# Start-up of a two-layer kernel: loads on two queues sorted by first use, the first tile's steps written ahead of the loops, weight pieces four tiles later, two accumulations of a pair tile in flight

## The reference

```python
x = x + attn(layernorm(x))     # delta-rule linear attention, 4 heads, key 128, value 64
x = x + ffn(layernorm(x))      # mixture of 8 experts, 2 chosen per token, hidden 1024
# attn: q, k = x@Wq, x@Wk; v, g = x@Wv, x@Wg; beta = sigmoid(x@Wb); k = k/|k|; q = q*128**-0.5
#   per token t: S = S + k_t (beta_t (v_t - k_t^T S))^T ; o_t = q_t^T S
#   o = rmsnorm(o) * norm_w * silu(g);  result o @ Wo
# ffn: probs = softmax(x @ router^T), top 2; sum over both of prob * gelu(x @ w1[e]^T) @ w2[e]^T
```

## Time and profile before

| | |
|---|---|
| median of three executions | 976.61 us (975.64 to 978.22) |
| profiled execution | 973.25 us, span 971.4 us |
| PE busy | 855.0 us (88%) |
| DVE busy | 628.9 us (65%) |
| ACT busy | 601.8 us (62%) |
| POOL busy | 425.5 us (44%) |
| mean granted TensorE clock | 0.962 of 2.4 GHz |

### The profile page before, as it was taken

The page is one execution under the profiler, slowest core; times in us unless marked ns, Lnnn a source line. Parts: engine busy times, 40 slices in busy tenths (PEclk is TensorE's granted clock), DMA queues, the critical chain, the costliest instruction groups (busy, mean ns, idle before and its releaser), DMA issues. The chain is left out here.

```text
span 971.4 us, 29866 instructions
## 1 busy us (share of the span) xinstructions
PE 855.0 (88%) x9998; PEld 671.8 (69%) x9999; DVE 628.9 (65%) x1822; ACT 601.8 (62%) x1636; POOL 425.5 (44%) x426
## 2 busy tenths in 40 slices
PE   0589999999999999999971699999999999998983
PEld 0368887788878877788751577777777777766762
DVE  3468888898989989898846354555555554534341
ACT  4578888898888888877642454455445544534430
POOL 3445555667767766754536023232323232222122
PEclk9999999999999999999965699999999999999997
DMA  5212222233233323211106123233232323222212
GB/s 196 66 50 87 64 73 89 79 100 100 84 96 99 106 82 92 88 46 46 46 34 220 56 39 48 47 53 51 44 49 44 59 44 50 45 46 41 39 18 28
DMA packets 49736, 66.58 MB, mean 69 GB/s; under 512 B 6416, under 2 KB 34192, under 8 KB 49616
## 3 DMA queue, kind: packets, MB, share of 16 engines
q1 hardware_dynamic: 35616, 46.33, 16.3%
q0 software_dynamic: 13424, 18.10, 10.7%
q10 hardware_dynamic: 576, 0.53, 0.2%
HBM read 41.46 MB, written 23.48 MB: 67 GB/s over the span
## 5 line engine op out<-in xcount | busy, mean ns | idle before, releaser
L646 POOL DMA_INDIRECT out<-wvg_s,yidx x71 | 113.7, 1601 | 317.7 <-DVE wvg_s L1911 169.0
L934 PE MATMUL ps<-w_s,wqk 128*128 128x128 f16 (+1 forms) x1336 | 240.0, 288 | 11.7 <-ACT wqk L663 9.0
L934 PE MATMUL ps<-x_s,w_hi 128*128 128x256 f16 (+1 forms) x1376 | 201.2, 256 | 0.1
L934 PE MATMUL ps<-x_s,w_lo 128*128 128x256 f16 (+1 forms) x688 | 170.2, 255 | 0.0
L1884 DVE SCALAR_TENSOR_TENSOR KpAT<-KQ,wqk 128x512 f16<-128x512 f32 (+1 forms) x144 | 98.7, 686 | 100.5 <-ACT wqk L663 100.4
L663 ACT ACTIVATE w_s<-ps 128x512 f16<-128x512 f32 (+2 forms) x288 | 147.8, 532 | 25.6 <-PE ps L934 10.4
L934 PE MATMUL ps<-w_s,KpAT 128*128 x568 | 155.7, 274 | 0.0
L934 PEld LDWEIGHTS ps<-w_s,wqk 128*128 128x128 f16 x1336 | 101.7, 98 | 77.9 <-issue 14.7
L934 PEld LDWEIGHTS ps<-x_s,w_hi 128*128 x1376 | 120.4, 98 | 18.4 <-issue 0.8
L663 ACT ACTIVATE x_s<-ps 128x512 f16<-128x512 f32 x36 | 21.5, 596 | 163.6 <-PE ps L1310 163.6
L910 ACT ACTIVATE KQ<-ps 128x512 f32<-128x512 f32 (+1 forms) x144 | 85.1, 591 | 48.1 <-PE ps L934 42.3
(11 more groups left out here) (185 smaller groups left out, 1792.0 us busy)
## 6 DMA issues: line engine op xcount, KB each, us to landing
wst<-w SPq DMA_DIRECT2D x56, 256.0 KB, 2.8
w_s<-eye SPq DMA_DIRECT2D x32, 256.0 KB, 2.7
rowA<-routed_rows SPq DMA_DIRECT2D x28, 260.0 KB, 2.7
x_s<-x SPq DMA_DIRECT2D x32, 128.0 KB, 2.6
out<-x_s SPq DMA_DIRECT2D x32, 128.0 KB, 1.7
rowA<-routed_rows SPq DMA_DIRECT2D x15, 130.0 KB, 2.1
KQ<-w SPq DMA_DIRECT2D x6, 256.0 KB
out<-wvg_s,yidx POOLq DMA_INDIRECT x71, 3.9
```

Source lines behind the costliest of these rows:

```text
L646: pool.indirect_dma_start(out=out, out_offset=bass.IndirectOffsetOnAxis(ap=yidx[:, q, a:a + 1], axis=0), in_=yrow[:, q % 2, a, :], in_offs ...
L934: return pe.matmul(dst, lhsT, rhs, start=start, stop=stop, **kw)
```

## The change

- Loads go out on two queues. ACT issues `wk` and `wvg` before anything else. SP issues x tile 0, `fc`, `wb`, `wq`, x tile 1, `norm_w` (once, repeated on the host), `wo`, the masks (int8 on the host, straight into place), identity block 0, x tile 2, `router`, three identity loads that fill `Y`, identity block 1, x tile 3, identity block 2.
- Each constant has a semaphore of its own, and each wait stands where it is first needed.
- The first tile's layer norm, its evacuation and the layer norm of tile 1 stand in the preludes, ahead of or between the weight parts. The spare rows are written in POOL's loop step 4.
- The weight order is wk, wq, wvg, wo. All piece steps are four loop steps later.
- The casts and scaled constants of DVE come after the low parts of wk and wq.
- In phase B, the first expert tile's `up` is cut in two around the second tile's transposes, and the second half of a pair tile no longer waits for its first half's accumulation.

```diff
@@ SP
             load_x(0)
-            for dst, src in early + late_consts:
-                sp.dma_start(dst, src).then_inc(s_const, 16)
-            for n, (dst, src) in enumerate(weights):
-                sp.dma_start(dst, src.rearrange("(k p) n -> p k n", p=P)).then_inc(s_wload[n], 16)
+            sp.dma_start(fc[:, 0:FCONST], fconst).then_inc(s_fc, 16)
+            sp.dma_start(wb_in[:, :, :], wb.rearrange("(k p) n -> p k n", p=P)).then_inc(s_wb, 16)
+            sp.dma_start(wq_in, wq.rearrange("(k p) n -> p k n", p=P)).then_inc(s_wload[1], 16)
             load_x(1)
+            sp.dma_start(normw_s[:, :], norm_w).then_inc(s_normw_in, 16)
+            sp.dma_start(wo_in, wo.rearrange("(k p) n -> p k n", p=P)).then_inc(s_wload[3], 16)
+            sp.dma_start(mask_s[:, :, :], iconst).then_inc(s_mask, 16)
+            init_inverse(0)
             load_x(2)
+            sp.dma_start(router_s[:, :, :], router.rearrange("(k p) n -> p k n", p=P)).then_inc(s_router, 16)
+            for n in range(RING):
+                sp.dma_start(Y[:, 2 * n:2 * n + 2, :, :].rearrange("p l h n -> p (l h n)"), eye).then_inc(s_Yi, 16)
+            init_inverse(1)
             load_x(3)
-            for n in range(RING):
-                init_inverse(n)
+            init_inverse(2)
...
-                piece(2 * (i - 2) + 1)
-                piece(2 * (i - 1) + 0)
+                piece(2 * (i - 6) + 1)
+                piece(2 * (i - 5) + 0)
@@ POOL
-            pool.memset(S[:, :, :, :], 0.0).then_inc(s_init, 1)
-            pool.wait_ge(s_const, 16 * CONST_LOADS)
+            pool.wait_ge(s_fc, 16)
...
+            ln1_scale(0)
+            ln1_scale(1)
             for i in range(T + POOL_SKEW):
+                if i == 4:
+                    spare_rows()
                 ln2_scale(i - 5)
-                split_lo(2 * (i) + 0)
+                split_lo(2 * (i - 4) + 0)
                 scatter(i - 12, 1)
-                ln1_scale(i)
+                next_scale(i)
...
-                    value = i * 128 + (32 * q + 16 * a)
+                    value = i * 128 + (32 * q + (16 * a if split(i, q) else 0))
@@ ACT
-            act.wait_ge(s_const, 16 * CONST_LOADS)
+            act.dma_start(wk_in, wk.rearrange("(k p) n -> p k n", p=P)).then_inc(s_wload[0], 16)
+            act.dma_start(wvg_in, wvg.rearrange("(k p) n -> p k n", p=P)).then_inc(s_wload[2], 16)
+            ln1(0)
+            act.wait_ge(s_wb, 16)
             evac(wb_s[:, 0, :, :], wb_in[:, :, :], A_SCALE)
-            evac(Y[:, :, :, :].rearrange("p v h n -> p (v h) n"),
-                 ident.unsqueeze(1).broadcast_to([P, (LEVELS - 1) * H, P])).then_inc(s_Yi, 1)
+            xnT_evac(0)
             weight_hi(0, wk_s[:, 0, :, :], wk_in)
-            weight_hi(1, wvg_s[:, 0, :, :], wvg_in)
-            weight_hi(2, wq_s[:, 0, :, :], wq_in)
+            weight_hi(1, wq_s[:, 0, :, :], wq_in)
+            ln1(1)
+            weight_hi(2, wvg_s[:, 0, :, :], wvg_in)
...
-                scale_piece(2 * (i - 1) + 0)
+                scale_piece(2 * (i - 5) + 0)
...
@@ PE
-            pe.wait_ge(s_const, 16 * CONST_LOADS)
-            pe.wait_ge(s_init, 2)
-            pe.wait_ge(s_Yi, 1)
-            pe.wait_ge(s_wsh, 1)
-            pe.wait_ge(s_wsl, 1)
+            pe.wait_ge(s_fc, 16)
...
             xT_make(0, 0)
+            up(0, 0, range(0, 4))
             xT_make(0, 1)
-            up(0, 0)
+            up(0, 0, range(4, KH))
@@ DVE
-            dve.wait_ge(s_const, 16 * CONST_LOADS)
-            dve.wait_ge(s_init, 1)
+            dve.wait_ge(s_fc, 16)
+            ln1_stats(0)
+            xnT_low(0)
+            weight_lo(0, wb_s, wb_in[:, :, :])
+            weight_lo(0, wk_s, wk_in).then_inc(s_wsl, 1)
+            ln1_stats(1)
+            dve.wait_ge(s_normw_in, 16)
+            dve.tensor_scalar(normw_s[:, :], normw_s[:, :], A_SCALE, None, ALU.mult).then_inc(s_normw, 1)
+            weight_lo(1, wq_s, wq_in).then_inc(s_wsl, 1)
+            step(dve.tensor_copy(posI[:, :], ident))
+            step(dve.tensor_scalar(negI[:, :], ident, -1.0, None, ALU.mult))
             step(dve.tensor_copy(before16[:, :], before_neg))
             step(dve.tensor_copy(ones16[:, :], ones))
-            step(dve.tensor_copy(posI[:, :], ident))
-            step(dve.tensor_scalar(negI[:, :], ident, -1.0, None, ALU.mult))
+            step(dve.tensor_copy(run[:, :], region))
             settled()
             step(dve.tensor_scalar(before_neg, before_neg, -K_SCALE ** -2, None, ALU.mult))
             step(dve.tensor_scalar(causal, causal, 1.0 / K_SCALE, None, ALU.mult))
-            dve.tensor_scalar(normw_s[:, :], normw_s[:, :], A_SCALE, None, ALU.mult).then_inc(s_normw, 1)
-            step(dve.tensor_copy(mask_s[:, :, :].rearrange("p a b -> p (a b)"), mask_in))
-            link(dve.tensor_copy(run[:, :], region))
+            settled()
             dve.sem_inc(s_init, 1)
-            ln1_stats(0)
-            dve.wait_ge(s_Yi, 1)
-            weight_lo(0, wb_s, wb_in[:, :, :])
-            weight_lo(0, wk_s, wk_in).then_inc(s_wsl, 1)
-            weight_lo(1, wvg_s, wvg_in).then_inc(s_wsl, 1)
-            weight_lo(2, wq_s, wq_in).then_inc(s_wsl, 1)
+            weight_lo(2, wvg_s, wvg_in).then_inc(s_wsl, 1)
             dve.wait_ge(s_normw, 1)
             weight_lo(3, wo_s, wo_in, normw_s[:, 0:1]).then_inc(s_wsl, 1)
```

More of the change, by code:

```diff
@@ L246, in build @@
         p_yo = [PS[5 + a][:, :].rearrange("p (v n) -> p v n", v=2) for a in range(2)]
-        s_const = sem("const_loaded")
-        s_wload = [sem(f"{n}_loaded") for n in ("wk", "wvg", "wq", "wo")]
+        s_fc = sem("constants_loaded")
+        s_wb = sem("wb_loaded")
+        s_mask = sem("level_masks_loaded")
+        s_router = sem("router_loaded")
+        s_normw_in = sem("norm_weight_loaded")
+        s_wload = [sem(f"{n}_loaded") for n in ("wk", "wq", "wvg", "wo")]
         s_wsh = sem("attention_weight_hi")
@@ L416, in _ @@
         def _(sp):
[L417 to L421, removed]
             def load_x(n):
@@ L613, in scatter, with spare_rows, next_scale @@
                     in_=rowA[:, g % RG * C + c, :], in_offset=None).then_inc(s_scat[g % RG][c], 16)
[L615 to L621, removed]
+            def spare_rows():
+                pool.memset(rowA[:, C:2 * C, :], 0.0).then_inc(s_spare, 1)
+                pool.wait_ge(s_spare, 1)
+                pool.tensor_scalar(rowA[:, C:2 * C, D + 3], rowA[:, C:2 * C, D + 3], lane, float(B * N), ALU.add, ALU.add).then_inc(s_spare, 1)
+                pool.wait_ge(s_spare, 2)
+                for c in range(C):
+                    part = c % 2 * 64
+                    pool.dma_start(routed[SPARE + 64 * c:SPARE + 64 * (c + 1), :], rowA[part:part + 64, C + c, :]).then_inc(s_spared, 16)
+            def next_scale(n):
+                if n > 1:
+                    ln1_scale(n)
+            ln1_scale(0)
+            ln1_scale(1)
             for i in range(T + POOL_SKEW):
+                if i == 4:
+                    spare_rows()
                 ln2_scale(i - 5)
-                split_lo(2 * (i) + 0)
+                split_lo(2 * (i - 4) + 0)
                 scatter(i - 12, 1)
-                ln1_scale(i)
+                next_scale(i)
                 o_rsqrt(i - 4)
-                split_lo(2 * (i) + 1)
+                split_lo(2 * (i - 4) + 1)
                 kscale_(i - 1)
@@ L898, in xT_hi, with hidden @@
                 evac(xTh[:, q % 2, :, :], p_gT).then_inc(s_gTh, 1)
-            def hidden(i, q):
-                for m in range(4):
+            def hidden(i, q, ms=range(4)):
+                for m in ms:
                     act.wait_ge(s_hps, i * 16 + (4 * q + m + 1))
@@ L914, in _ @@
             xT_hi(0, 0)
+            hidden(0, 0, range(0, 2))
             xT_hi(0, 1)
-            hidden(0, 0)
+            hidden(0, 0, range(2, 4))
             def expert_body(i):
@@ L1323, in parts_of, with up @@
                 return [(expert_of(i, q), slice(0, PE_TOK))]
-            def up(i, q):
+            def up(i, q, ms=range(KH)):
                 owners = parts_of(i, q)
@@ L1329, in up @@
                 hi, lo = xTh[:, q % 2, :, :], xTl[:, q % 2, :, :]
-                for m in range(KH):
+                for m in ms:
                     if m % 2 == 0 and not (isinstance(i, int) and i * 4 + q < 1):
@@ L1507, in y_masked @@
                 done(dve, s_yps[q], n // 2, 7, lev + 1)
+                if n == 0 and lev == 1:
+                    dve.wait_ge(s_Yi, 16 * RING)
                 hold(dve)
@@ L1813, in _ @@
                 expert_masks(i - 8)
-                xnT_low(i - 2)
+                next_xnT_low(i - 2)
                 v_gate(i - 3)
@@ L1878, in xT_lo, with hidden_lo @@
                 dve.tensor_tensor(xTl[:, q % 2, :, :], p_gT, xTh[:, q % 2, :, :], ALU.subtract).then_inc(s_gTl, 1)
-            def hidden_lo(i, q):
-                for m in range(4):
+            def hidden_lo(i, q, ms=range(4)):
+                for m in ms:
```

(5 more changed lines are left out.)

47 lines of the change are left out of this document (31 added, 16 removed).

## The result

The changed kernel took 963.22 us (961.45 to 965.0, four runs), the kernel before 977.34 us in the same comparison: 14.1 us less, ratio 0.9853 [0.9832, 0.9874]. The forecast was 960.9. In two later comparisons, on other chips, the changed kernel took 968.56 us against 980.80 and 969.36 against 979.73, ratios 0.9876 [0.9861, 0.9891] and 0.9898 [0.9881, 0.9916]. So 10 to 14 us is the gain, and the forecast's 15.7 us is above all three.

What follows compares the result with a forecast made beforehand. TensorE was taken as nearly full within both phases and empty mainly at the start, where tile 0 queued behind weight pieces. Terms -14.9 - 1.0 + 0.2 = -15.7 us took the median 976.61 to 960.9, range 955 to 967.

Steps and rivals of the forecast that it cites:

- the signs that the prediction set itself: Trace marks: first projection 11 to 12 us, Gram product 23 to 25, DVE idle near nothing, last beta_proj 15 to 17 earlier.
- The first tile's path: Start, tile 0 from fc's landing: statistics at 5.5 us, first projection at 11.4 in place of 28.35, 16.9 us earlier.
- What is late next: Before tile 0's key scale: DVE's prelude delays k_norm(0) from 16.6 to 18.6, giving back 2.0 us (0.5 to 3.3).
- Gain at the first Gram product: 16.9 - 2.0 = 14.9 us.: Start: first projection's 16.9 us lead less 2.0 given back at the key scale; k', transposes and Gram products follow.
- The early tiles without pieces: Early phase A, 38.6 to 74 us: less piece work ahead of the inverse's steps gains 1.0 us (0 to 4).
- rival (a): Early iterations gain too, PE's idle between 38.6 and 74 us shrinking by 4 us or more: 957 us; chance 0.17.
- the spare rows: POOL's loop step 4: moved there at cost 0, covered since only kscale_(3) waits behind; 3.8 us if cover is gone.
- Pieces at the end of phase A: Pieces stop four steps later, at step 32 of 39: 0.2 us lost (0 to 1).
- Expert phase: Phase B: swapped expert start 0 (up to 0.5 either way), overlapped accumulations 0.
- Rival (b): Gain partly lost in a new line (late loads, DVE's prelude, spare rows), 4 to 6 us less: 966 us; chance 0.15.
- (c): Phase B: two accumulations in flight hinder each other, slower; 993 us if a pair takes 12.0 us; chance 0.02.
- (d): Start doesn't move, something after it holds the pipeline; time within 3 us of 976.6; chance 0.02.

Runs made afterwards that it cites:

- one_queue: Changed kernel with all loads on SP's queue, wk after wb and wvg after x tile 1, none on ACT's: 968.43 us, ratio 0.9873.
- shift_only: Kernel before with only the weight pieces' steps moved four loop steps later: 965.85 us against 975.76, ratio 0.9885.
- start_all: Changed kernel with all loads on SP's queue, spare rows in POOL's prelude, and less work before tile 0's key scale: 965.67 us, ratio 0.9867.
- start_all_warm: start_all plus unread matmuls (5, 8, 8 and 4) in PE's idle of the start: 961.54 us, ratio 0.9819.
- no_shift: Changed kernel with the weight pieces back at their old loop steps, all else kept: 978.14 us, ratio 1.0025.
- phase_b_undone: Changed kernel with the expert phase edits taken back (first up in one piece, every accumulation waits for the one before): 963.38 us, ratio 0.9858.
- warm: Changed kernel with unread matmuls added at the start (8 before and 8 after the first transposes, 16, then 4): 967.79 us, ratio 0.9878.
- before_second: The kernel before, unchanged, profiled a second time: 980.09 us, ratio 1.0009.

## Why the prediction came out as it did

Direction and range held, and so did the mechanism of the first tile's path; the gain was sized 1.6 us too large against the first comparison and 5 us against the last. That 963.2 is so near to 960.9 is in part luck. Of the signs that the prediction set itself, the first projection (11.75) came true; the first Gram product at 25.65 missed 23 to 25, DVE had an idle of 1.40 us where nearly none was expected, and the last `beta_proj` came at 465.01, 8.0 us earlier and not 15 to 17 (4.5 to 11.8 us over the six pairs of executions of the two kernels). The marks show 9.3 to 11.5 us at tile 4, and nothing after it was changed by an amount that these runs can tell.

- The first tile's path: right to 0.4 us. Forecast 5.5 for the statistics, measured 5.54; forecast 11.4 for the first projection, measured 11.75. Each term could be taken from before, because the instructions are the same and only their waits went. `fc` paid for the second queue, 1.1 us by one_queue, 0.9 forecast.
- What is late next: the right engine, DVE, and 0.65 us too little. `k_norm(0)` came at 19.25, forecast 18.6. The small steps took 1.1 us (13.46 to 14.57) where I had 1.4. What I didn't have: POOL's power of tile 1 (the step that makes 1/sqrt of its variance) took 1.55 us, where it takes 0.58 alone, beside DVE's low part of wq from 12.33. ACT's norm, wvg's high part and DVE's low part of wvg (1.40 idle) were all late by that 1.0 us. The page "SBUF — State Buffer" of the Trainium skill, section "Who interferes with whom", says that a DVE instruction with two SBUF inputs contends with a GpSimd one that reads SBUF; the rows agree with that, and so does shift_only, where POOL's two steps of tile 0 ran beside DVE's low parts and took 1.45 and 1.78 us (0.58 and 0.26 in the changed kernel). The experiment that would separate it wasn't made.
- The step that failed: "Gain at the first Gram product: 16.9 - 2.0 = 14.9 us." It lets k', its transposes and the Gram products follow with PE's durations of before. In before, the key transposes and the wvg projection ran at the fast level, 0.63 and 1.46 us; after, at the slow one, 1.08 and 2.77: PE runs at 1.2 GHz from about 20 to 27 us. That is 1.35 us at the first Gram product, which with the 0.65 of `k_norm(0)` makes up the 2.0 us that are missing there (12.97 measured, 14.9 forecast), and more by tile 4: 3.3 us in the pair start_all and start_all_warm. That PE had idled 4.08 us just before, in place of 2.50, doesn't explain it alone: in shift_only and no_shift it had idled 2.51 and 2.25 us and the same matmuls ran at the slow level too (1.09 and 2.69, 1.08 and 2.77), in start_all_warm 2.71 us and they ran at the fast one. What the pair shows is that more work of PE ahead of this idle keeps the clock; why before kept it with so little isn't shown.
- The early tiles without pieces: forecast a gain of 1.0, measured a loss, so rival (a) fell as well. From the Gram product to tile 4 the lead shrank from 13.0 to 9.4 us, in the later executions to about 11. Two terms are known: the spare rows, counted at 0 with 3.8 if the cover were gone (measured 1.3 us in the step from tile 2 to 3 without a fall of the clock), and the clock. The cover I named, `kscale_(3)`, did have room; it was `ln1_scale(4)`, also behind them, that hadn't.
- Pieces at the end of phase A: 0.2 us were forecast; no more than the scatter of the steps (385 to 391 us for 27) can be told.
- Expert phase: 0 forecast, nothing measured that the 3 us of phase_b_undone's interval can tell.

Rival (b), part of the gain lost in a new line, describes what happened better than the forecast does: 4 to 6 us less, spare rows among its causes. I gave it 0.15. Rivals (c) and (d) fell with phase_b_undone and shift_only.

What stays open: why single steps between tiles 4 and 31 take 15 to 17 us in some executions and not in others, and why the transition takes from 67.3 to 71.7 us. Both occur in either kernel. The clock explains few of these steps: it was under 1.00 in only 4 of the 378, three of them 16.0 to 16.9 us long, and all others over 15 us had it at 1.00.

## What to carry to other kernels

When an engine's program holds background work with a period of its own, here a load cycle of 5 us through one buffer, every step written behind it inherits that period until the pipeline is full; move the background behind the fill before anything else is polished. For a step moved into the loop, list all that is queued behind it on its engine, not the one consumer that comes to mind. And compare marks inside the trace, here one per tile, rather than spans: the profiled spans differed by 9.4 us, the runs by 14, the part that was changed by 9.3 to 11.5.

## What the runs showed of the hardware

- TensorE's granted clock fell to its slow level in the sparse start of every kernel but warm, before (0.88 from tile 1 to tile 2) included. 25 unread matmuls kept it at 1.00 until 32 us, worth 4.1 us of 965.7; 36 of them, with the other waits still there, kept it for 70 us and showed no gain.
- Ahead of the first fall the clock column isn't to be relied on: it reads 1.00 from the start of the span, but the first projection, six matmuls of 512 columns, took 2.72 us in before and in the changed kernel, and 1.45 and 1.46 us after unread matmuls. Durations say more there.
- The time from the first expert transposes to the first matmul at the fast level varied from 5.9 (no_shift) to 8.8 us (before_second) among fourteen executions, in before (8.2 and 8.8) as in the changed kernel (6.4, 8.3 and 8.4).
- Two indirect accumulations of 128 rows in flight go out 1.86 us apart in place of 4.65, and cost POOL little more: the mean of all 71 issues is 1.68 us in the changed kernel, 1.58 in phase_b_undone, where each waits for the one before.
